# Position bias MLP of a deformable attention: its third layer for two groups of tiles at once, every second time

## The reference

```
pos  = grid_q[:, :, None, :] - grid_kv[:, None, :, :]        # 16 x 1024 x 64 x 2
bias = sign(pos) * log1p(abs(pos))
bias = relu(bias @ cpb_w1 + cpb_b1)                          # 2 -> 128
bias = relu(bias @ cpb_w2 + cpb_b2)                          # 128 -> 128
bias = (bias @ cpb_w3 + cpb_b3)                              # 128 -> 1
```

## Time and profile before

| | |
|---|---|
| median of three runs | 4471.59 us (4470.86 to 4475.02) |
| the profiled execution | 4470.45 us |
| its span, first to last instruction | 4468.6 us |
| TensorE busy | 3954.4 us (88%) |
| VectorE busy | 2971.8 us (67%) |
| ScalarE busy | 2532.4 us (57%) |
| GpSimd busy | 1223.0 us (27%) |
| mean granted clock of TensorE | 0.936 |

### The profile page before, as it was taken

How to read it: one execution, slowest core, us unless ns; L and a number is a source line. 1 busy time by engine, 2 the same in 40 slices (tenths; PEclk the granted TensorE clock), 3 DMA queues, 4 the chain that set the end, 5 groups by cost and what they waited for, 6 DMA issues and landing times. The chain is left out here.

```text
span 4468.6 us, 65255 instructions
## 1 busy us (share of the span) xinstructions
PE 3954.4 (88%) x19432; PEld 2398.8 (54%) x19432; DVE 2971.8 (67%) x4247; ACT 2532.4 (57%) x4506; POOL 1223.0 (27%) x848
## 2 busy tenths in 40 slices
PE   2599999999999999999998999669878356969999
PEld 1355555555555555555555777537666232435553
DVE  7777777777777777777776333366888944235552
ACT  3488888888888888888885333222211220113331
POOL 1411111111111111111111445405667610016663
PEclk7799999999999999999999999889889666989999
DMA  1200000000000000000002000118999821363311
GB/s 44 86 2 2 2 2 2 2 2 2 2 2 2 2 2 2 2 2 2 2 2 77 1 0 0 65 41 320 377 376 374 309 82 49 125 155 67 67 39 76
DMA packets 136115, 309.13 MB, mean 69 GB/s; under 512 B 43400, under 2 KB 44424, under 8 KB 135004
## 3 DMA queue, kind: packets, MB, share of 16 engines
q1 hardware_dynamic: 94556, 157.02, 11.3%
q0 software_dynamic: 41472, 151.01, 8.7%
HBM read 228.83 MB, written 78.91 MB: 69 GB/s over the span
## 5 line engine op out<-in xcount | busy, mean ns | idle before, releaser
L572 DVE SCALAR_TENSOR_TENSOR cpb_r<-cpb_z,cpb_r 128x512 fp32r<-128x512 f32 x2052 | 1321.8, 686 | 491.8 <-ACT cpb_r L547 486.0
L547 ACT ACTIVATE cpb_r<-cpb_z 128x512 fp32r<-128x512 f32 x2052 | 1121.1, 604 | 278.0 <-PE cpb_z L479 278.0
L553 ACT ACTIVATE cpb_h<-cpb_z,net_vec 128x512 f32<-128x512 f32 x1536 | 1020.5, 714 | 2.0 <-PE cpb_z L495 2.0
L492 PE MATMUL cpb_z<-cpb_r,cpb_w2a 128*128 128x512 f32 x2048 | 856.7, 418 | 3.0
L493 PE MATMUL cpb_z<-cpb_r,cpb_w2b 128*128 128x512 f32 x2048 | 803.6, 392 | 0.0
L495 PE MATMUL cpb_z<-cpb_r,cpb_w2a 128*128 128x512 f32 x2048 | 797.4, 389 | 0.0
L430 POOL TENSOR_TENSOR cpb_exp<-l0k_posx,l0k_pos 128x1024 bf16 (+1 forms) x130 | 247.6, 1905 | 1966.3 <-PE cpb_z L479 1947.0
L1365 DVE SCALAR_TENSOR_TENSOR dc_acc<-dc_g,dc_wt,dc_acc 128x512 f32<-128x512 f32 x560 | 459.2, 826 | 52.4 <-DMA dc_g<-conv_out,dc_idx 36.9
L492 PEld LDWEIGHTS cpb_z<-cpb_r,cpb_w2a 128*128 128x128 f32 x2048 | 384.1, 188 | 189.8 <-issue 123.3
L504 PE MATMUL cpb_zo<-cpb_h,cpb_w3w 128*32 128x512 f32 x3584 | 477.3, 605 | 0.0
L495 PEld LDWEIGHTS cpb_z<-cpb_r,cpb_w2a 128*128 128x128 f32 x2048 | 385.3, 188 | 85.3
(11 more groups left out here) (320 smaller groups left out, 4884.8 us busy)
## 6 DMA issues: line engine op xcount, KB each, us to landing
conv_out<-dc_ys SPq DMA_DIRECT2D x576, 64.0 KB, 6.2
qk_parts<-gn_r SPq DMA_DIRECT2D x64, 256.0 KB, 2.0
dc_wr<-in_dc_wT SPq DMA_DIRECT2D x9, 1024.0 KB, 5.9
bias_dram<-cpb_bst SPq DMA_DIRECT2D x520, 8.0 KB
net_x<-in_x SPq DMA_DIRECT2D x8, 1024.0 KB, 8.7
sa_qa<-qk_parts SPq DMA_DIRECT2D x16, 512.0 KB
sa_ka<-qk_parts SPq DMA_DIRECT2D x16, 512.0 KB
dc_g<-conv_out,dc_idx POOLq DMA_INDIRECT x288, 7.9
```

The lines of the kernel that those rows point to most:

```text
L492: pe.matmul(z2[:, bank, :], W2A[:], R1[:, k, :], start=True, stop=False)
L547: act.activation(R1[:, t % RING, :], z1[:, t % 4, :], ACT.Relu).then_inc(r1_ready, 1)
L553: act.activation(H2[:, t % 8, :], z2[:, t % 3, :], ACT.Relu, bias=V("cpb_b2")).then_inc(h2a, 1)
L572: v.scalar_tensor_tensor(R2[:, t % RING, :], z1[:, t % 4, :], 0.0, R1[:, t % RING, :].bitcast(F32), ALU.max, ALU.subtract).then_inc(r2_rea ...
```

## The change

Layer3 is no longer done in each quad. In quads 3, 5 and 7 TensorE does it for two quads, q - 3 and q - 2, one right behind the other; in quad 1 for the last two of the iteration before (`last_quads`); in quads 0, 2, 4 and 6 not at all. Operands have to be kept longer, so `H2` has sixteen slots in place of eight, and the zeros that stand for quads before the first fill eight slots in place of four. The counts of `h2_free` follow, and `read_out` goes from quad 0 to quad 2. The zeroing matmuls before the loop stay four.

```
-        H2 = s.sb("h2", [P, 8, NF])
+        H2 = s.sb("h2", [P, 16, NF])
...
-            pool.memset(H2[:, 4:8, :], 0.0).then_inc(win_zero, 1)
+            pool.memset(H2[:, 8:16, :], 0.0).then_inc(win_zero, 1)
             pool.sem_inc(stored, 16)
-            pool.sem_inc(h2_free, 1)
+            pool.sem_inc(h2_free, 2)
...
-                    mm = pe.matmul(zo[32 * r:32 * r + 32, :], W3W[:, half * 4 + c, :], H2[:, (quad * 4 + r) % 8, :],
+                    mm = pe.matmul(zo[32 * r:32 * r + 32, :], W3W[:, half * 4 + c, :], H2[:, (quad * 4 + r) % 16, :],
                                    start=(quad == 0), stop=False)
                 mm.then_inc(h2_free, 1)

-            def last_quad(i):
-
-                pe.wait_ge(h2a, by_act(i, -1))
-                pe.wait_ge(h2v, by_vector(i, -1))
-                for r in range(4):
-                    mm = pe.matmul(zo[32 * r:32 * r + 32, :], W3W[:, 7, :], H2[:, 4 + r, :], start=False, stop=True)
-                mm.then_inc(h2_free, 1)
+            def last_quads(i):
+
+                for quad in (QUADS - 2, QUADS - 1):
+                    pe.wait_ge(h2a, by_act(i, quad * 4 + 3 - TPI))
+                    pe.wait_ge(h2v, by_vector(i, quad * 4 + 3 - TPI))
+                    half, _, _, c = quad_of(quad)
+                    for r in range(4):
+                        mm = pe.matmul(zo[32 * r:32 * r + 32, :], W3W[:, half * 4 + c, :], H2[:, (quad * 4 + r) % 16, :],
+                                       start=False, stop=(quad == QUADS - 1))
+                    mm.then_inc(h2_free, 1)
...
-                pe.matmul(zo[32 * r:32 * r + 32, :], W3W[:, 7, :], H2[:, 4 + r, :], start=True, stop=False)
+                pe.matmul(zo[32 * r:32 * r + 32, :], W3W[:, 7, :], H2[:, 12 + r, :], start=True, stop=False)
...
-                    if quad == 0:
-                        last_quad(i)
-                    else:
-                        layer3(i, quad - 1)
+
+                    if quad == 1:
+                        last_quads(i)
+                    elif quad % 2:
+                        layer3(i, quad - 3)
+                        layer3(i, quad - 2)
...
-            last_quad(ITERS)
+            last_quads(ITERS)
...
-                act.activation(H2[:, t % 8, :], z2[:, t % 3, :], ACT.Relu, bias=V("cpb_b2")).then_inc(h2a, 1)
+                act.activation(H2[:, t % 16, :], z2[:, t % 3, :], ACT.Relu, bias=V("cpb_b2")).then_inc(h2a, 1)
...
-                v.wait_ge(h2_free, i * QUADS + 2)
+                v.wait_ge(h2_free, i * QUADS + 4)
...
-                    v.tensor_scalar(H2[:, (t + 2) % 8, :], z2[:, (t + 2) % 3, :], V("cpb_b2"), 0.0, ALU.add, ALU.max
+                    v.tensor_scalar(H2[:, (t + 2) % 16, :], z2[:, (t + 2) % 3, :], V("cpb_b2"), 0.0, ALU.add, ALU.max
                                     ).then_inc(h2v, 1)
-                    if t == 0:
+                    if t == 8:
                         read_out(i)
```

## The result

The changed kernel takes 4617.83 us (median of 4 runs, 4612.85 to 4618.81), the one before on the same chips 4471.23 (4 runs). The ratio is 1.0322, 95% interval 1.0306 to 1.0338: slower by 146.6 us. 4623 was forecast, within 4608 to 4680.

What follows compares the result with a forecast made beforehand. The prediction took TensorE to bound the bias stage. A pair of quads going from 8.53 to 9.11 us made 2.35 us an iteration, times 64: 150.4, plus 2.6, 153 on 4470.45: 4623 us, range 4608 to 4680.

Steps and rivals of the forecast that it cites:

- The wait that takes the place of layer3: Even quads: without layer3, TensorE's layer1 waits for the last R2; quad 3.97 us, 0.71 us of it idle.
- case (a): The forecast itself: even quads wait for R2, odd quads are bound by TensorE; 4623 us, own range 4608 to 4649, 74%.
- Reading L572 in the table of waits as no bound: Kernel before: layer1's weight load shows 391.6 us waiting for VectorE's L572, but layer1 really waits for layer3's matmuls.
- The odd quad: TensorE, layer1 to layer1 with two layer3: 3.26 + 0.88 + 1.00 = 5.14 us.
- Rival (b): Odd quads: the two layer3 don't join up, the second costs 1.00 us or more; 4654 to 4680 us, 14%.
- the 0.10 us at the loop's end: Last quad of each iteration: a delay of 0.10 us that also delays hidden and R2, kept in the changed kernel.
- the iteration before: Loop of the kernel before: 34.19 us for each of 64 iterations, 7 x 4.26 + 4.37.
- Set-up and end: Outside the loop: +1.8 us once for the longer H2 memset, +0.8 for a second layer3 after the loop.
- The sum: Whole loop: 36.54 us an iteration against 34.19, 2.35 more, times 64; with 2.6 us for the rest, +153 us.
- Rival (c): Even quads: TensorE stays the bound at 3.26 us, a pair of quads is 8.40 us; 4442 us, faster, 4%.
- Rival (d): TensorE's clock falls because of 256 holes of 0.7 us; 123 us on top, 4746 us, 4%.

Runs made afterwards that it cites:

- the filler: Three zero-weight matmuls added in each even quad: to the changed kernel, 4621.33 us (ratio 1.0335); to the kernel before, 4647.55 us (ratio 1.0396).
- the halves of R1 and R2: Only 256 of 512 columns made: changed kernel, R2 alone 4523.21 us, R1 and R2 4458.76 us; kernel before, R1 and R2 4470.41 us.
- the even spacing: Changed kernel with two layer2 tiles of the odd quad before the even quad's layer1, hidden shared otherwise and made earlier: 4463.90 us, ratio 0.9980.

## Why the prediction was right

- **The wait that takes the place of layer3** (case (a)): right in place, cause and size. 3.97 us were forecast for the even quad, 3.98 measured; 3.92 us to the last R2 in both traces. That it is a wait of TensorE for R2, and the whole loss, is shown by the filler (some 4 us in all here, 176 us in the order before), by the halves of R1 and R2, and by the even spacing, which with the whole computation brings the time back. The idle time was put at 0.71 us each and some 180 in all. The table of waits has 0.60, 154 us for 256 of them, since a matmul counts as busy past the start of the next; by starts the hole is 3.98 - 3.31 = 0.67.
- **Reading L572 in the table of waits as no bound**: right. With VectorE and ScalarE relieved, the kernel before gained nothing (0.9998).
- **The odd quad**: 5.14 forecast, 5.12 to 5.17 measured. Its parts are off in opposite ways: 0.86 for the second layer3 where I had 0.88 (and 0.87 as the least), 3.26 to 3.32 up to the first (3.29 on average) where I had 3.26. Rival (b), 1.00 or more for it, is out. The Trainium skill's rule that loads overlap running matmuls only where the row group differs (TensorE: Matmul & The Clock Gate, The mechanism) would have led to (b), and the trace disagrees again: the second group's loads run under the first group's matmuls, on the same rows. The same section also lets loads into the background weight buffer go ahead of running matmuls; with that the trace agrees. With what the Trainium skill says of a change of tiling mode, that it drains the engine (TensorEngine Tiling (Array Packing), Key Properties), it agrees in so far as layer3 to layer1 takes 1.00 us and layer3 to layer3 0.86; no run shows that it is the drain.
- **Wrong, the 0.10 us at the loop's end.** I took it for a delay of the loop that also holds hidden and R2 up, and kept it in the changed kernel (6.4 us). In the trace before, L492 starts at 1008.64, 0.14 us after VectorE's hidden of tile 30 ends (1007.76 + 0.74 = 1008.50): tiles 30 and 0 share a bank of z2 two tiles apart. In the changed kernel layer2 follows layer1 by 0.32 to 0.33 us in every quad from 300 to 2300 us: the last quad of an iteration is odd, its layer1 comes some 0.9 us later than before, and VectorE's hidden is over by then. In the old order with half of R1 and R2 this quad is as long as the others. That it is the bank, and not something else that a faster VectorE relieves, is argued from the times.
- **Mis-sized, the iteration before**: 34.19 us was counted up to the layer3 behind the loop, which has no layer2 before it; 34.24 is right, 3 us in all. That 7 x 4.26 + 4.37 gave the same 34.19 was an accident of rounding: the quads are 4.27 us (4.267) on average.
- **Set-up and end**: +2.6 us forecast. The memset did grow (1.80 to 3.51 us), but quad 0 of the first iteration no longer has a layer3; from the start of GpSimd's L430 (174.20 us; 174.94 before) to layer1 it is 15.79 us against 15.94, and the end is 0.73 us longer: +0.6 together.
- The sum: 36.51 an iteration measured, 36.54 forecast, 36.51 - 34.24 = 2.27 instead of 2.35. The errors, 3 + 6.4 + 2 us one way and some 5 us the other (a pair of 9.13 and not 9.11), are the 6 us between the +153 of the forecast and the +146.6 of the result.
- **Rival (c)**, TensorE remaining the bound, was wrong in the place where it had to hold and over-stated besides: with the path to R2 shortened the joined layer3 are worth 12 us, and with nothing left out 4. **Rival (d)** is out: granted clock 1.00 from 300 to 2300 us.

## What to carry to other kernels

Work that is taken out between two steps of a pipeline may be what covers the path between them: measure from the step's start to the end of what it waits for (3.92 us here, against a period of 4.26), and compare that with the new, uneven periods, not with the mean. In the table of waits, a wait of the weight loads for an engine says little (391.6 us of it before, with TensorE busy for 1997.2 of 2000); a wait of TensorE itself is a hole. And if work is moved to cover a path, look whether the path runs through what it is put in front of: here two R1 stood behind hidden in ScalarE's written order, and the path to the last R2 grew by 0.9 us.

## What the hardware showed that was not expected

From layer1 to layer3, with layer2's twelve matmuls between them, it takes 3.26 to 3.27 us in every quad in the order before and 3.31 in every odd quad in the new order, though nothing waited there and the shapes are the same (the two kernels with half of R1 and R2, 300 to 2300 us). Twice in a pair, it ate more than half of the 0.13 us that one switch of tiling less seemed to give: a pair is 8.48 us where it was 8.53. In the changed kernel itself the same stretch takes anything from 3.26 to 3.32. No run here says where it comes from.
